# The softmax normalisation emitted two key tiles earlier, and a contiguous view for the exp, in an eight-core transformer layer

## The chip, the cores and the metric

The kernel runs on the 8 NeuronCores of one Trainium2 chip. Each core computes one sequence of 2048 tokens by 1024 features, and the cores exchange nothing. The metric is the device time in microseconds (us) of the slowest core, and the median over several executions is what counts.

## The reference

The reference adds four residual stages to x, each behind a layer norm: a holographic attention with cosines and sines (stage A), a product with the signs of a weight, a causal softmax attention with 16 heads of 64 (stage B), and the product with signs again. The change touches only stage B:

```python
Q = (x @ Wq.T + bq).reshape(b, t, H, D).transpose(0, 2, 1, 3)
K = (x @ Wk.T + bk).reshape(b, t, H, D).transpose(0, 2, 1, 3)
V = (x @ Wv.T + bv).reshape(b, t, H, D).transpose(0, 2, 1, 3)
wei = jnp.einsum('bhqd,bhkd->bhqk', Q, K) * (1.0 / math.sqrt(D))
wei = jnp.where(causal, wei, -jnp.inf)
att = jax.nn.softmax(wei, axis=-1)
out = jnp.einsum('bhqk,bhkd->bhqd', att, V)
out = out.transpose(0, 2, 1, 3).reshape(b, t, c) @ Wo.T + bo
x = x + out
```

Here t is 2048, c is 1024, H is 16 and D is 64.

## The kernel before

Everything lies transposed, with features on the 128 partitions and tokens along the free axis: XT holds x in float32, LNT the normed x in bf16, BIG the attention's output in bf16. Each stage is a function that appends instructions to a list for each engine (`Builder.op`), and the lists are emitted as they stand. There is no scheduler: the order in which the Python code calls `b.op` is the order in which each engine works, and an instruction whose semaphore has not come holds up all that stands behind it on its engine. VectorE, ScalarE and GpSimd also wait for their own instruction before.

Stage B (`emit_attnb`) takes the 16 heads as 8 pairs, p = 0 to 7, two heads one above the other on the partitions. In a pair it walks 4 query blocks of 512 queries (qs), and in a block the key tiles of 128 keys (kt): 4, 8, 12 and 16 of them, two at a time (kc). For one key tile there are:

- the scores S: two matmuls, K times Q of the two heads, into the PSUM tile PC (even kt) or PD (odd kt) (lines 890 and 895; on the diagonal also the mask, lines 902 and 904);
- the exp: one ScalarE activation of both heads, from PC or PD into one of four SBUF buffers (`do_exp`, line 934);
- the product AV: two matmuls with 64 columns of V and a column of ones, which accumulate over kt in PO0 and PO1, the two halves of the PSUM tile POB (lines 867 and 871). The column of ones makes row 64 the softmax's denominator.

AV of a pair of key tiles is issued two key tiles later than its scores. A query block ends with its last AVs. Then comes its norm (`make_norm`): for each of the two heads a Ln of the denominator (line 955) and an Exp of its negative (line 960) on ScalarE, a copy of the 64 output rows from PSUM to SBUF on VectorE (line 965), a TensorE matmul that spreads the reciprocal over 64 partitions, into the PSUM rows just copied (line 969), and the product of both into BIG (line 976). A copy of one row (line 986) closes it, and the first AV of the next block waits for that, since it writes PO0 and PO1 again. The norm is not emitted when its block ends but kept in `pending_norm` and called inside the next block's loop, in the iteration kc = 2. The norm of the very last block is called after it.

Between the scores and the AVs of each iteration one unit of the next pair's projections is issued (`make_qkv_units`), 25 in a pair: a memset of the V buffer (line 757), 4 units of Q and 4 of K (8 matmuls of 512 columns each, lines 766 and 789, evacuated by VectorE at lines 776 and 800), and 16 units of V (9 matmuls of 128 columns, lines 812 and 818, evacuated at line 827). A pair has 20 iterations. The five units left over follow its last block. Then GpSimd issues the weight loads for the pair after the next (`plan_w`, through line 214). The unit right behind the scores of kc = 0 is called U1 below, and the one of kc = 2 is U2. Where a pair changes, U1 is the memset and U2 is the first Q unit, Q0. Pair 7 has no units.

So there are 31 changes from a query block to the next: 14 in pairs 0 to 6 where U1 and U2 are Q or K units (qs 0 to 1 and 1 to 2), 7 in the same pairs where they are V units (qs 2 to 3), 6 changes of pair up to pair 6 with weights just ordered, the change from pair 6 to 7, and 3 inside pair 7.

Of the kernel before, what the change touches and what calls it, by code (L numbers as in the profile page):

```python
# [10 lines left out]
AF = mybir.ActivationFunctionType  # L11
# [64 lines left out]
def build_program(stop_after=None):  # L76
# [34 lines left out]
    with contextlib.ExitStack() as stack:  # L111
# [610 lines left out]
        def emit_attnb(ln_toks):  # L722
# [121 lines left out]
            pending_norm = [None]  # L844
            for p in range(NB):
# [5 lines left out]
                for qs in range(4):  # L851
# [5 lines left out]
                    def plan_av(kt, qs=qs, nkt=nkt, VSB=VSB,  # L857
                                av_toks=av_toks):
                        diag = kt >= 4 * qs
                        qoff = 128 * kt if diag else 512 * qs  # L860
                        N = (512 * (qs + 1) - 128 * kt) if diag else 512
                        ep = (EPA, EPB, EPC, EPD)[kt % 4]

                        def mm_av(t, kt=kt, qs=qs, ep=ep, qoff=qoff, N=N,
                                  nkt=nkt, VSB=VSB):
                            o = qoff - 512 * qs
                            t.matmul(PO0[0:65, o:o + N],  # L867
                                     VSB[:, kt * 130:kt * 130 + 65],
                                     ep[:, 0:N],
                                     start=(kt == 0), stop=(kt == nkt - 1))  # L870
                            return t.matmul(  # L871
                                PO1[0:65, o:o + N],
                                VSB[:, kt * 130 + 65:kt * 130 + 130],
                                ep[:, 512:512 + N],
                                start=(kt == 0), stop=(kt == nkt - 1))
                        wav = [exp_toks[kt]]
                        if kt == 0 and norm_done is not None:
                            wav.append(norm_done)
                        av_toks[kt] = b.op("tensor", mm_av, wait=wav,
                                           sem="T", inc=1)  # L880

                    for kc in range(0, nkt, 2):
                      for kt in (kc, kc + 1):
                        diag = kt >= 4 * qs
                        qoff = 128 * kt if diag else 512 * qs
                        N = (512 * (qs + 1) - 128 * kt) if diag else 512
                        ps = PC if kt % 2 == 0 else PD
                        def mm_s(t, ps=ps, kt=kt, qoff=qoff, N=N, diag=diag,
                                 QTp=QTp, KTp=KTp):
                            t.matmul(ps[:, 0:N],  # L890
                                     KTp[0:64, kt * 128:kt * 128 + 128],
                                     QTp[0:64, qoff:qoff + N],
                                     start=True, stop=not diag,
                                     tile_position=(0, 0))
                            ins = t.matmul(  # L895
                                ps[:, 512:512 + N],
                                KTp[64:128, kt * 128:kt * 128 + 128],
                                QTp[64:128, qoff:qoff + N],
                                start=True, stop=not diag,
                                tile_position=(64, 0))  # L900
                            if diag:
                                t.matmul(ps[:, 0:128], IDENTB[:], MASKB[:],
                                         start=False, stop=True)
                                ins = t.matmul(ps[:, 512:640], IDENTB[:],
                                               MASKB[:], start=False,
                                               stop=True)
                            return ins
                        w = list(qt_all)
                        if kt >= 2:
                            w.append(exp_toks[kt - 2])  # L910
                        elif prev_qs_exp is not None:
                            w.append(prev_qs_exp)
                        ts_ = b.op("tensor", mm_s, wait=w, sem="T", inc=1)
                        exp_toks.append([ts_, None])
                      if pending_norm[0] is not None and kc >= 2:
                          norm_done = pending_norm[0]()
                          pending_norm[0] = None
                      if pending:
                          pending.pop(0)()
                      while avq and avq[0] <= kc - 1:  # L920
                          plan_av(avq.pop(0))
                      for kt in (kc, kc + 1):
                        diag = kt >= 4 * qs
                        qoff = 128 * kt if diag else 512 * qs
                        N = (512 * (qs + 1) - 128 * kt) if diag else 512
                        ps = PC if kt % 2 == 0 else PD
                        ep = (EPA, EPB, EPC, EPD)[kt % 4]
                        wexp = [exp_toks[kt][0]]
                        if kt >= 4:
                            wexp.append(av_toks[kt - 4])  # L930
                        elif prev_qs_av is not None:
                            wexp.append(prev_qs_av)
                        def do_exp(s, ps=ps, ep=ep, N=N):
                            return s.activation(  # L934
                                ep.rearrange("p (h n) -> p h n", h=2)
                                [:, :, 0:N],
                                ps[:].rearrange("p (h n) -> p h n", h=2)
                                [:, :, 0:N], AF.Exp)
                        te = b.op("scalar", do_exp, wait=wexp, sem=None,
                                  inc=0)  # L940
                        exp_toks[kt] = te
                        avq.append(kt)
# [63 lines left out]
        for si in range(stop_idx):  # L1006
            st = STAGES[si]
            if st.startswith("ln"):
                ln_out = emit_ln(done)
                done = ln_out  # L1010
            elif st == "attna":
                done = emit_attna(ln_out)
            elif st == "ffn1" or st == "ffn2":
                done = emit_ffn(ln_out, out_dma=(st == "ffn2"))
                if st == "ffn2":
                    streamed_out[0] = True
            elif st == "attnb":
                done = emit_attnb(ln_out)
# [84 lines left out]
```

How the kernel before makes its waits and increments, by code:

```python
            def run(eng):  # L49
                hi = {}
                chain_pos = {}
                for fn, waits, sem, inc, chain in self.events[eng_name]:
                    if chain:
                        k = chain_pos.get(chain, 0)
                        if k > 0:
                            eng.wait_ge(sems[chain], k)
                        chain_pos[chain] = k + 1
                    for ws, wv in waits:
                        if wv > 0 and hi.get(ws, 0) < wv:
                            eng.wait_ge(sems[ws], wv)
                            hi[ws] = wv
                    ins = fn(eng)
                    if inc:
                        ins.then_inc(sems[sem], inc)
                    elif chain:
                        ins.then_inc(sems[chain], 1)
                return None
```

## Time and profile before

| What | us |
|---|---|
| median of 2 executions | 1731.24 (1730.67 to 1731.81) |
| the profiled execution | 1732.45 |
| its span, slowest core (core 2) | 1730.9 |
| spans of the 8 cores | 1723.2 to 1730.9 |
| stretch of stage B's attention on core 2 | some 835 to 1530 |

The span runs from the first to the last instruction of a core. The mean granted TensorE clock of the cores is 0.773 to 0.783 of full speed. PE is TensorE's matmuls, ACT is ScalarE, DVE is VectorE, POOL is GpSimd and SP is SyncE. In rows of the timeline the columns are: start in us, duration in us, engine, line, operation, output and inputs, count, and in brackets the engine's idle time before it with what ended it.

### The profile page before, as it was taken

What the parts mean: (1) busy time and instruction counts of PE and PEld (TensorE: products, weight loads), DVE (VectorE), ACT (ScalarE), POOL (GpSimd) and SP (SyncE); (2) the same over time, 40 slices, a digit from 0 to 9 for tenths busy, and PEclk for the clock granted to TensorE, in tenths of its full rate; (3) what the DMA queues carried; (4) which work ended last, traced back from release to release, by engine and by line L of the source; (5) the groups of instructions that cost most, each with busy time, mean ns of one, the idle gap of its engine ahead of it and who ended that gap; (6) DMA issues with size and microseconds to landing.
All of it is one profiled execution on the core that took longest, in us unless ns stands there. A gap on an engine that the chain in (4) does not pass through costs nothing.

```text
span 1730.9 us, 16268 instructions; the slowest of 8 cores (1723.2 to 1730.9 us)
## 1 busy us (share of the span) xinstructions
PE 1020.3 (59%) x5088; PEld 432.3 (25%) x5088; DVE 835.7 (48%) x1072; ACT 640.9 (37%) x747; POOL 56.9 (3%) x69
## 2 busy tenths in 40 slices
PE   0434343432311942961887877787878787677458
PEld 0111111110100410420433333333333333233123
DVE  1466888888898337336422223232322222125453
ACT  0535423343220051042154555554545555611400
POOL 1000000000000100001000000000000000010000
PEclk9767677675655975975988888887888887788679
DMA  9003112311000400102102020202020200022025
GB/s 244 0 1 30 23 20 37 36 12 12 0 7 6 37 1 12 37 0 26 12 1 19 1 19 1 19 1 19 1 19 1 19 1 1 1 25 25 0 64 180
DMA packets 73156, 42.03 MB, mean 24 GB/s; under 512 B 67696, under 2 KB 67696, under 8 KB 71024
## 3 DMA queue, kind: packets, MB, share of 16 engines
q0 software_dynamic: 66592, 16.78, 10.8%
q1 hardware_dynamic: 6480, 24.21, 4.5%
q8 instruction: 43, 0.70, 0.2%
q14 instruction: 41, 0.34, 0.1%
HBM read 47.28 MB, written 10.49 MB: 33 GB/s over the span
## 4 chain that ended last, share of the span: by engine, by line
PE 43%; DVE 30%; ACT 14%; issue 5%; DMA 5%; DVEq 1%; SPq 1%; POOL 1%; ACTq 0%; POOLq 0%
PE PC L624 7%; PE PC L692 5%; ACT POOLBF L934 5%; PE POB L867 4%; PE PRB L766 4%; PE POB L871 4%; PE PRB L812 3%; DVE LNT L379 3%; DVE POOLBF L374 3%; PE PRB L789 3%; ACT POOLBF L262 3%; PE PD L498 2%; DVE POOLBF L568 2%; DVE POOLBF L562 2%; DVE POOLBF L550 2%
## 5 line engine op out<-in xcount | busy, mean ns | idle before, releaser
L934 ACT ACTIVATE POOLBF<-PC 128x1024 bf16<-128x1024 f32 (+1 forms) x160 | 150.1, 938 | 308.9 <-PE PC L895 157.3
L262 ACT ACTIVATE POOLBF<-LNT 128x2048 bf16<-128x2048 bf16 x32 | 61.1, 1910 | 235.4 <-DVE LNT L256 231.3
L934 ACT ACTIVATE POOLBF<-PD 128x1024 bf16<-128x1024 f32 (+2 forms) x160 | 136.4, 853 | 24.1 <-PE PRB L818 0.4
L867 PE MATMUL POB<-POOLBF 128*65 128x512 bf16 (+1 forms) x320 | 123.8, 392 | 9.2 <-DVE PF L986 9.2
L827 DVE CAST POOLBF<-PRB 128x128 bf16<-128x128 f32 x128 | 37.7, 295 | 187.2 <-PE PRB L818 185.9
L871 PE MATMUL POB<-POOLBF 128*65 128x512 bf16 (+1 forms) x320 | 118.2, 385 | 0.0
L498 PE MATMUL PD<-LNT,WSB 128*128 128x512 bf16 x128 | 39.1, 474 | 93.5 <-ACT POOLBF L506 93.5
L283 PE MATMUL POB<-LNT,ONESB 128*1 128x512 bf16 x128 | 41.7, 485 | 86.3 <-DVE LNT L256 86.3
L624 PE MATMUL PC<-BIG,WSA 128*128 128x512 bf16 x256 | 61.4, 401 | 45.6 <-DVE BIG L580 39.9
L969 PE MATMUL POB<-PF,ONESRB 1*64 1x512 bf16 x64 | 32.5, 509 | 92.7 <-DVE PF L965 53.3
L976 DVE TENSOR_TENSOR BIG<-PF,POB 64x512 bf16<-64x512 f32 x64 | 43.5, 680 | 87.2 <-PE POB L969 87.2
L692 PE MATMUL PC<-LNT,WSA 128*128 128x512 bf16 x256 | 64.1, 413 | 22.1 <-DVE XT L702 14.0
L702 DVE TENSOR_TENSOR XT<-XT,PC 128x512 f32<-128x512 f32 x64 | 44.0, 688 | 68.3 <-PE PC L692 67.6
L498 PE MATMUL PD<-LNT,WSA 128*128 128x512 bf16 x128 | 36.1, 446 | 68.3 <-ACT POOLBF L506 68.3
L890 PE MATMUL PC<-POOLBF 64*128 64x512 bf16 (+1 forms) x160 | 61.3, 383 | 16.8 <-ACT POOLBF L934 11.6
L776 DVE TENSOR_SCALAR POOLBF<-PRB,DER 128x512 bf16<-128x512 f32 x32 | 24.0, 751 | 95.9 <-PE PRB L766 95.6
L344 PE MATMUL PRB<-PF,ONESRB 1*128 1x512 bf16 x16 | 8.5, 531 | 104.5 <-ACT PF L336 104.5
L458 PE MATMUL PC<-LNT,WSA 128*128 128x512 bf16 x128 | 41.6, 497 | 48.1 <-DMA WSA<-wv 25.8
L458 PE MATMUL PC<-LNT,WSB 128*128 128x512 bf16 x128 | 41.7, 500 | 43.6 <-DMA WSB<-wv 25.9
L890 PE MATMUL PD<-POOLBF 64*128 64x512 bf16 (+2 forms) x160 | 56.7, 355 | 16.8 <-ACT POOLBF L934 15.5
L965 DVE COPY PF<-POB 64x512 f32<-64x512 f32 x64 | 43.7, 683 | 43.7 <-PE POB L871 37.6
L895 PE MATMUL PC<-POOLBF 64*128 64x512 bf16 (+1 forms) x160 | 61.7, 385 | 0.0
(144 smaller groups left out, 2022.3 us busy)
## 6 DMA issues: line engine op xcount, KB each, us to landing
XT<-xT SPq DMA_DIRECT2D x8, 1024.0 KB, 17.5
yT<-XT SPq DMA_DIRECT2D x8, 1024.0 KB, 5.2
BIG<-wts POOLq DMA_DIRECT2D x8, 256.0 KB, 7.1
wsgn<-BIG SPq DMA_DIRECT2D x8, 256.0 KB, 2.3
WSA<-wsgn SPq DMA_DIRECT2D x8, 256.0 KB, 4.0
WSB<-wsgn SPq DMA_DIRECT2D x8, 256.0 KB, 4.4
WSA<-wk POOLq DMA_DIRECT2D x4, 256.0 KB, 5.5
WSA<-wv POOLq DMA_DIRECT2D x4, 256.0 KB, 7.3
```

Source lines behind the costliest of these rows:

```text
L262: tk = b.op("scalar", lambda s, cb=cb: s.activation(SQF[:, cb * T:(cb + 1) * T], LNT[:, cb * T:(cb + 1) * T], AF.Square), wait=[copy_toks[ ...
L374: v.tensor_tensor(SQF[:, sl], LNT[:, sl], RB[:, s4 * 512:s4 * 512 + 512], ALU.mult), wait=[e2])
L458: ins = t.matmul(PC[:, (s4 % 2) * 512:(s4 % 2) * 512 + 512], ws[:, i * 128:i * 128 + 128], LNT[:, i * T + s4 * 512: i * T + s4 * 512 + 512 ...
L498: ins = t.matmul(PD[:, (s4 % 2) * 512:(s4 % 2) * 512 + 512], ws[:, 1024 + i * 128:1024 + i * 128 + 128], LNT[:, i * T + s4 * 512:i * T + s ...
L624: ins = t.matmul(PC[:, (s4 % 2) * 512:(s4 % 2) * 512 + 512], ws[:, i * 128:i * 128 + 128], BIG[:, i * T + s4 * 512:i * T + s4 * 512 + 512] ...
L692: ins = t.matmul(PC[:, (s4 % 2) * 512:(s4 % 2) * 512 + 512], ws[:, i * 128:i * 128 + 128], LNT[:, i * T + s4 * 512:i * T + s4 * 512 + 512] ...
L766: ins = t.matmul(prr[:], ws[:, i * 128:i * 128 + 128], LNT[:, i * T + s4 * 512: i * T + s4 * 512 + 512], start=(i == 0), stop=(i == NB - 1))
L867: t.matmul(PO0[0:65, o:o + N], VSB[:, kt * 130:kt * 130 + 65], ep[:, 0:N], start=(kt == 0), stop=(kt == nkt - 1))
L871: return t.matmul(PO1[0:65, o:o + N], VSB[:, kt * 130 + 65:kt * 130 + 130], ep[:, 512:512 + N], start=(kt == 0), stop=(kt == nkt - 1))
L890: t.matmul(ps[:, 0:N], KTp[0:64, kt * 128:kt * 128 + 128], QTp[0:64, qoff:qoff + N], start=True, stop=not diag, tile_position=(0, 0))
L895: ins = t.matmul(ps[:, 512:512 + N], KTp[64:128, kt * 128:kt * 128 + 128], QTp[64:128, qoff:qoff + N], start=True, stop=not diag, tile_pos ...
L934: return s.activation(ep.rearrange("p (h n) -> p h n", h=2) [:, :, 0:N], ps[:].rearrange("p (h n) -> p h n", h=2) [:, :, 0:N], AF.Exp)
```

## The change

It has two parts. The condition `kc >= 2` goes, so that the pending norm of a block is emitted in the iteration kc = 0 of the next: behind the first two scores and ahead of U1, and on ScalarE ahead of the first two exps. And where a key tile has all 512 queries, the exp is written over `ep[:, 0:1024]` and `ps[:, 0:1024]` in place of a view with the two heads as a dimension of their own. Lines behind the second edit move by 5: in the kernel after, 934 becomes 935 or 939, 955 becomes 960, 960 becomes 965, 965 becomes 970, 969 becomes 974, 976 becomes 981 and 986 becomes 991.

```diff
-                      if pending_norm[0] is not None and kc >= 2:
+                      if pending_norm[0] is not None:
                           norm_done = pending_norm[0]()
                           pending_norm[0] = None
                       if pending:
...
-                        def do_exp(s, ps=ps, ep=ep, N=N):
-                            return s.activation(
-                                ep.rearrange("p (h n) -> p h n", h=2)
-                                [:, :, 0:N],
-                                ps[:].rearrange("p (h n) -> p h n", h=2)
-                                [:, :, 0:N], AF.Exp)
+                        if N == 512:
+                            def do_exp(s, ps=ps, ep=ep):
+                                return s.activation(
+                                    ep[:, 0:1024], ps[:, 0:1024], AF.Exp)
+                        else:
+                            def do_exp(s, ps=ps, ep=ep, N=N):
+                                return s.activation(
+                                    ep.rearrange("p (h n) -> p h n", h=2)
+                                    [:, :, 0:N],
+                                    ps[:].rearrange("p (h n) -> p h n", h=2)
+                                    [:, :, 0:N], AF.Exp)
```

**TensorE, change from qs 2 to qs 3.** Before, behind the first two scores of the new block, TensorE's row holds U1 (a V unit), the next two scores, the norm's two matmuls, U2 and the first AV:

```order
L812 MATMUL PRB<-WSB,LNT 128x128 x8
L818 MATMUL PRB<-BVR,ONESRB 128x128
L890 MATMUL PC<-POOLBF 128x512
L895 MATMUL PC<-POOLBF 128x512
L890 MATMUL PD<-POOLBF 128x512
L895 MATMUL PD<-POOLBF 128x512
L969 MATMUL POB<-PF,ONESRB 64x512 x2
L812 MATMUL PRB<-WSB,LNT 128x128 x8
L818 MATMUL PRB<-BVR,ONESRB 128x128
L867 MATMUL POB<-POOLBF 65x512
```

The same place after the change:

```order
L974 MATMUL POB<-PF,ONESRB 64x512 x2
L812 MATMUL PRB<-WSB,LNT 128x128 x8
L818 MATMUL PRB<-BVR,ONESRB 128x128
L890 MATMUL PC<-POOLBF 128x512
L895 MATMUL PC<-POOLBF 128x512
L890 MATMUL PD<-POOLBF 128x512
L895 MATMUL PD<-POOLBF 128x512
L812 MATMUL PRB<-WSB,LNT 128x128 x8
L818 MATMUL PRB<-BVR,ONESRB 128x128
L867 MATMUL POB<-POOLBF 65x512
```

The norm's two matmuls have moved ahead of U1 and of the scores of kt = 2 and 3. Nothing else moved, and nothing stands between them and U1.

**ScalarE, change from one block to the next (here into qs 2).** Before, from the last exp of the old block (a tile of 128 queries, both heads) on:

```order
L934 ACTIVATE POOLBF<-PD 128x2x128
L934 ACTIVATE POOLBF<-PC 128x1024
L934 ACTIVATE POOLBF<-PD 128x1024
L955 ACTIVATE PF<-POB 1x512
L960 ACTIVATE PF<-PF 1x512
L955 ACTIVATE PF<-POB 1x512
L960 ACTIVATE PF<-PF 1x512
L934 ACTIVATE POOLBF<-PC 128x1024
```

After:

```order
L939 ACTIVATE POOLBF<-PD 128x2x128
L960 ACTIVATE PF<-POB 1x512
L965 ACTIVATE PF<-PF 1x512
L960 ACTIVATE PF<-POB 1x512
L965 ACTIVATE PF<-PF 1x512
L935 ACTIVATE POOLBF<-PC 128x1024
L935 ACTIVATE POOLBF<-PD 128x1024
L935 ACTIVATE POOLBF<-PC 128x1024
```

The four activations of the norm have moved ahead of the new block's first two exps. The exps of full tiles stand as 128x1024 in both.

**VectorE, change of pair.** Before, from the last V casts of the old pair's iterations over the five left over to the first Q evacuations of the new one:

```order
L827 CAST POOLBF<-PRB 128x2x64 x12
L757 MEMSET POOLBF 128x2080
L965 COPY PF<-POB 64x512
L976 TENSOR_TENSOR BIG<-PF,POB 64x512
L965 COPY PF<-POB 64x512
L976 TENSOR_TENSOR BIG<-PF,POB 64x512
L986 COPY PF<-PF 1x512
L776 TENSOR_SCALAR POOLBF<-PRB,DER 128x512 x2
```

After:

```order
L827 CAST POOLBF<-PRB 128x2x64 x13
L970 COPY PF<-POB 64x512
L981 TENSOR_TENSOR BIG<-PF,POB 64x512
L970 COPY PF<-POB 64x512
L981 TENSOR_TENSOR BIG<-PF,POB 64x512
L991 COPY PF<-PF 1x512
L757 MEMSET POOLBF 128x2080
L776 TENSOR_SCALAR POOLBF<-PRB,DER 128x512
```

The memset has moved behind the norm's five operations; the thirteenth cast is that of qs 3's first iteration, which used to stand ahead of the norm before it.

## Rows read from the trace of the kernel before

**Rows 1.** The page: span, and granted TensorE clock in 40 slices.
```profile
span 1730.9 us, 16268 instructions; the slowest of 8 cores (1723.2 to 1730.9 us)
...
PEclk9767677675655975975988888887888887788679
```
**Rows 2.** Busy time by windows, attention of stage B (window: us, busy by engine, PEclk).
```profile
835.00:1530.00 695.00, 540.31 (x3224) 243.47 (x3221) 195.91 (x355) 364.39 (x448) 17.55 (x20) 0.83 0.08 8
```
**Rows 3.** Waits in 850 to 1525 (who, for whom: us, times, longest).
```profile
PE POB L969 <- DVE PF L965: 51.6, 30, 1.7
PE POB L969 <- ACT PF L960: 37.4, 32, 1.7
```
**Rows 4.** Timeline, pair 1, change from qs 2 to qs 3.
```profile
989.91 0.22 PE L871 MATMUL POB<-POOLBF 128*65 128x128 bf16 x1
...
990.55 1.02 ACT L934 ACTIVATE POOLBF<-PC 128x1024 bf16<-128x1024 f32 x1 [1.39 <-PE PC L895]
...
992.83 0.59 ACT L955 ACTIVATE PF<-POB 1x512 f32<-1x512 f32 x1
...
992.89 0.37 PE L890 MATMUL PD<-POOLBF 64*128 64x512 bf16 x1 [0.78 <-ACT POOLBF L934]
...
994.45 0.37 PE L969 MATMUL POB<-PF,ONESRB 1*64 1x512 bf16 x1 [1.17 <-ACT PF L960]
...
996.55 0.60 PE L969 MATMUL POB<-PF,ONESRB 1*64 1x512 bf16 x1 [1.72 <-DVE PF L965]
...
997.08 1.03 PE L812 MATMUL PRB<-WSA,LNT 128*128 128x128 bf16 x8
...
998.74 0.61 PE L867 MATMUL POB<-POOLBF 128*65 128x512 bf16 x1 [0.41 <-DVE PF L986]
```
**Rows 5.** Timeline, the norm behind the very last block.
```profile
1521.46 0.22 PE L871 MATMUL POB<-POOLBF 128*65 128x128 bf16 x1
...
1523.39 0.37 PE L969 MATMUL POB<-PF,ONESRB 1*64 1x512 bf16 x1 [1.71 <-ACT PF L960]
...
1525.48 0.60 PE L969 MATMUL POB<-PF,ONESRB 1*64 1x512 bf16 x1 [1.72 <-DVE PF L965]
```
**Rows 6.** Timeline, pair 1, change from qs 1 to qs 2.
```profile
967.84 0.22 PE L871 MATMUL POB<-POOLBF 128*65 128x128 bf16 x1
...
968.53 1.90 PE L789 MATMUL PRB<-LNT,WSA 128*128 128x512 bf16 x8
...
975.29 3.21 PE L789 MATMUL PRB<-LNT,WSA 128*128 128x512 bf16 x8
...
978.34 0.38 PE L867 MATMUL POB<-POOLBF 128*65 128x512 bf16 x1
```
**Rows 7.** Busy time by windows, the same place (PEclk is the third number from the end).
```profile
968.00:974.00 6.00, 3.51 (x19) 1.12 (x17) 2.18 (x4) 4.48 (x6) 0.00 (x0) 1.00 0.01 3
974.00:978.00 4.00, 3.24 (x8) 1.16 (x9) 1.71 (x3) 2.05 (x2) 0.00 (x0) 0.57 0.02 4
```
**Rows 8.** Timeline, change from pair 1 to pair 2.
```profile
1020.27 1.79 DVE L757 MEMSET POOLBF<- 128x2080 bf16 x1 [0.57 <-DVE POOLBF L827]
...
1020.83 0.22 PE L904 MATMUL PD<-MASKB,IDENTB 128*128 128x128 bf16 x1
...
1021.57 0.90 POOL L214 DMA_DIRECT2D WSB<-wvbT  x1
...
1026.66 0.60 PE L969 MATMUL POB<-PF,ONESRB 1*64 1x512 bf16 x1 [1.72 <-DVE PF L965]
...
1029.70 3.30 PE L766 MATMUL PRB<-LNT,WSB 128*128 128x512 bf16 x8 [2.44 <-DMA WSB<-wvbT]
```
**Rows 9.** Timeline, pair 7, change from qs 2 to qs 3.
```profile
1496.79 0.22 PE L871 MATMUL POB<-POOLBF 128*65 128x128 bf16 x1
...
1505.84 0.61 PE L867 MATMUL POB<-POOLBF 128*65 128x512 bf16 x1 [1.59 <-DVE PF L986]
```
**Rows 10.** Groups of ACT by line and shape.
```profile
L934 ACT ACTIVATE POOLBF<-PC 128x1024 bf16<-128x1024 f32 x128 | 131.0, 1023 | 287.8 <-PE PC L895 157.3 <-PE PC L904 124.9
```

## The prediction, written before the changed kernel ran

> **What bounds the kernel now.** I read the page first, then the busy time by windows of stage B's attention, its waits, and last the timeline around single changes of query block. The page gives a span of 1730.9 us and shows TensorE's granted clock at 0.8 or 0.9 in most slices of the stage [rows 1]. The stage takes 695 us: TensorE is busy 540 us of it, ScalarE 364 us, and the mean clock is 0.83 [rows 2]. Since the clock has two levels, 1.2 and 2.4 GHz, 0.83 means that the lower one holds for about a third of the stage. So TensorE is the bound, and it loses time by idling and by the low clock that follows. Where does it idle? The waits name the norm's matmul: 51.6 us for VectorE's copy and 37.4 us for ScalarE's Exp, 89 us together in 62 waits [rows 3]. That is the largest idle time of TensorE in the stage, and the change moves just this piece.
>
> The timeline shows why one norm costs so much. Take the change of pair 1 from qs 2 to qs 3 [rows 4]. The last AV starts at 989.91 and ends its columns at 990.13, which I call +0. ScalarE then starts two exps (the first at +0.4), and the Ln of the norm stands behind them and starts only at +2.7, though the sums that it reads were there at +0. The norm's first matmul starts at +4.3, the second at +6.4, and the next AV at +8.6. The two matmuls are 2.1 us apart because VectorE copies the second head only after it has multiplied the first, and the AV is 2.2 us behind the second matmul because it waits for the closing copy (line 986), not for data. On this core 6 of the 7 changes with V units take 8.6 us from AV to AV, one 8.5; the 14 with Q or K units take 10.0 to 10.7, as the one at 968.06 does (978.34 less 968.06 is 10.3) [rows 6].
>
> **The exp's view.** The order of instructions shows the full tiles as 128x1024 before and after, so the old view was already folded into one row of 1024 elements. It takes 1023 ns before [rows 10]. I cost this edit at 0. As bounds I take 20 ns either way on each of the 224 full tiles, 4.5 us if all of them lay on the path; they do not, as ScalarE has 330 us of slack in the stage [rows 2].
>
> **The norm moved.** What does it take without the two exps ahead of it? The trace has that case: behind the very last block the norm is called at once. AV ends at 1521.68 (start 1521.46 and 0.22), and the matmuls start at 1523.39 and 1525.48, so at +1.7 and +3.8 in place of +4.3 and +6.4 [rows 5]. The norm is 2.6 us earlier. But U1 and the scores of kt = 2 and 3, which used to fill TensorE while the exps and the Ln ran, now stand behind it. What counts is TensorE's idle time between the last AV and the next, kind by kind. I count it from where a matmul has taken in its columns (0.22 us for 512 of them at 2.4 GHz, the distance of two AVs), not from the end that the row shows (0.37), since the next can start there.
>
> *14 changes with Q or K units.* Before, TensorE works to about +3.0 (two scores 0.45, U1 1.8, two scores), with 0.24 idle between the last two scores. It idles 1.3 to the first matmul at +4.3 and 1.9 to the second, 3.45 in all. After, it works to +0.5, idles 1.2 to +1.7 and 1.9 to +3.8, 3.1 in all, and then U1, scores and U2 follow without a gap: the exps of kt = 0 and 1, now behind the norm on ScalarE, end by +5.2 (four activations to +3.0, two exps of 1.1), while U1 ends at +6 or later. The gain is 0.33 us each, 4.6 us. Bounds: with both units at 2.4 GHz AV would start at 3.8 + 0.2 + 1.75 + 0.45 + 1.75 = +7.95, a gain of 2.3; with both at 1.2 GHz at 3.8 + 0.4 + 3.4 + 0.85 + 3.4 = +11.9, a loss of 1.6. One of two units is slow now (1.90 against 3.21 us [rows 6]), so I stay near the idle account.
>
> *7 changes with V units.* V units are short, so the exps lie open today. TensorE idles 0.4 and 1.0 ahead of the scores of kt = 2 and 3, which wait for an exp each (0.78 for the second by the row's own count), 1.3 and 1.9 ahead of the norm's matmuls, and 0.4 ahead of AV: 5.1 in all [rows 4]. After, idle is again 3.1. The gain is about 1.95 us each. Worked by AV's start, the V unit takes 1.2 us slow (997.08 to 998.3, line 812 and the bias behind it) and 0.7 fast: 3.8 + 0.4 + 1.2 + 0.85 + 1.2 = +7.5 slow. Fast it would be +5.9, and there the closing copy decides at 3.8 + 2.2 = +6.0. Against +8.6 this is 1.1 to 2.6 us [rows 4]. I take 1.9, 13.3 us.
>
> *3 changes in pair 7.* There are no units, so AV follows the closing copy: +6.0 for a change whose AV now starts at 1505.84 less 1497.01 = +8.8 [rows 9]. 2.7 us each, 8.1 us; half of it if the exps take it back.
>
> *The change from pair 6 to 7.* Like pair 1 to 2, but without a load to wait for. Ln and Exp are done while the five left-over V units run. The first scores end at 1021.05 and the first matmul follows, the second 2.1 us later at 1023.2 in place of 1026.66 [rows 8]. That is 3.5 us once; the two scores that follow take about 1 us and fit in the 2.2 us of the closing copy.
>
> *6 changes of pair.* There Q0 waits for its weights: the load is issued at 1021.57, behind the last left-over unit, and lands for 1029.70, with TensorE idle 2.44 us [rows 8]. The norm gets 3.5 us earlier and TensorE waits that much longer for the same load. Nothing is gained; what hides the edit is the transfer. GpSimd's row is not moved past anything.
>
> The wait that the change adds is that of the norm's matmuls ahead of U1. Behind them stand U1, two scores and U2; VectorE's evacuation of U1 waits with them, but the next unit writes the other half of PRB, so it holds nobody.
>
> **Sum.** 4.6 + 13.3 + 8.1 + 3.5 + 0 = 29.5 us. The profiled execution took 1732.45 us, 1.55 more than its span and 1.2 more than the median. 1732.45 less 29.5 is 1703; less 1.2, so that it compares with the median of 1731.24, 1702.
>
> **The clock.** It is full to about 974.5 and at its lower level until about 978 (0.57 as a mean over 974 to 978) [rows 7]: after the two idle times of the norm TensorE runs a few us of its work at 1.2 GHz. The idle pattern after the change is the same as in the Q and K cases, and more compact in the V cases and in pair 7. So I value the clock at 0, but it is the main unknown: a slow stretch that is longer or shorter by 3.4 us of busy time (the 974.5 to 978 piece) is worth 1.7 us at each of 24 changes. The Trainium skill's page "TensorE: Matmul & The Clock Gate", section "HAM oscillation — how this bites in real kernels", says that idle gaps throttle the array and that the work behind them then starts cold, again and again. The trace agrees, with 3.21 us for a unit behind the gap and 1.90 ahead of it. By that rule alone U1 and both scores, now behind the gap, would be slow as well, which is the third case below.
>
> **The rivals.**
>
> - *The clock gains too.* The idle pieces of V changes and of pair 7 come closer together and the slow stretch gets shorter by 3.4 us in half of the 24 changes and a bit more: 14 times 1.7 is 24 more, 1678. For it: the V changes idle 5.1 us now and 3.1 after. Against it: the Q and K changes have hardly less idle time.
> - *The clock takes it back.* U1, the scores and U2 all run at 1.2 GHz in the 14 Q and K changes, 1.7 us each: 29.5 less 24 leaves 6, 1726. For it: there is now more work right behind the gap. Against it: what ran slow behind U2 before is fast instead.
> - *The exps bind.* ScalarE's order between AVs is full with 4 activations and 4 exps, and the V blocks and pair 7 are near its rate of one exp in 1.1 to 1.2 us. Half of 13.3 and 8.1 is lost: 1713.
> - *Slower than before.* In all 24 changes the slow stretch grows by one piece of 3.4 us of busy time: 24 times 1.7 is 41, less 29.5 is 11 more, 1743. It decides once 17 or more of them grow so. It would take two such pieces each to pass 2%.
> - *The loads land earlier.* At a change of pair the memset (1020.27 to 1022.06) now lies beside GpSimd's issues and after the change behind the norm [rows 8]. If it had held the issues up, six loads would come up to 1.8 us earlier: 11 more, 1691. The Trainium skill's page "SBUF — State Buffer", section "SBUF: two separate sides", says that a VectorE operation in a two-port mode keeps GpSimd from writing descriptors. The trace does not show it: the issue beside the memset takes 0.90 us like the others.
>
> **How the numbers follow.** Forecast 0.47, clock gains 0.22, clock takes back 0.13, exps bind 0.10, slower 0.05, loads earlier 0.03. About 2% is what a measurement of this kernel can tell from no change; that is 34.6 us, so "faster" starts below 1696.6. The forecast's own spread is some 10 us, and a quarter of it (0.11) lies there; with the 0.22 and most of the 0.03 it makes 0.35. Slower by over 2% is the tail of one case, 0.02, which leaves 0.63 for within 2%. The range goes from 1684, between the forecast and the clock's gain, to 1724, near the case in which the clock takes it back.
>
> **What would show it.** Right: the norm's matmuls at +1.7 and +3.8 behind the last AV, AV to AV at about 10.0 (Q, K), 7 (V) and 6.0 (pair 7), Q0 waiting for its weights 4 to 6 us in place of 2.4, a mean clock still near 0.83 over the stage, exps at 1023 ns. Wrong: matmuls later than that (another wait has taken over), a clock away from 0.83 by more than 0.02, changes of pair that get shorter, or a gap ahead of the scores of kt = 2 and 3 that waits for an exp.

## The result and the profile after

The kernel after takes 1709.2 us (median of 7, 1705.9 to 1713.0) against 1731.6 us (median of 6, 1729.6 to 1732.8) for the kernel before on the same chip. The ratio is 0.9872 with a 95% interval of 0.9857 to 0.9886: 22 us or 1.3% faster. The forecast was 1702, range 1684 to 1724. In some executions of these programs the cores of one die run at a lower clock and take some per cent longer; they count in the medians given here and not in the ratios.

The head of the page and the granted clock in 40 slices, of the kernel after; they answer to [rows 1]:

```profile
span 1710.7 us, 16270 instructions; the slowest of 8 cores (1683.3 to 1710.7 us)
...
PEclk9867677675655985975897888887878788788679
```

The clock looks as before. What is new is in the first line: the cores lie 27 us apart, where it was 8 us before. The list of the cores' spans of the same execution (core: span, mean clock):

```profile
core 0: 1710.6 us, clock 0.776
core 1: 1710.7 us, clock 0.773
core 2: 1683.3 us, clock 0.784
core 3: 1692.3 us, clock 0.779
...
core 6: 1710.7 us, clock 0.780
```

Over the 8 executions of the kernel after with spans for each core, the mean of all cores is 1697.5 us, and the slowest and the fastest core of an execution are 21.7 us apart on average. Over 30 executions of the kernel before, on the three chips of the later runs, they are 1725.5 and 8.7 us. So a core gains 28 us on average, and the slowest of eight, which is the metric, gains 22. Which cores are slow changes from one execution to the next.

The timeline of the change from qs 2 to qs 3 in pair 2 on core 6, which has the longest span; it answers to [rows 4]. The last AV of the old block ends at 1068.95:

```profile
1068.88 0.39 PE L890 MATMUL PC<-POOLBF 64*128 64x512 bf16 x1
...
1069.05 0.59 ACT L960 ACTIVATE PF<-POB 1x512 f32<-1x512 f32 x1 [1.06 <-PE POB L871]
...
1070.67 0.37 PE L974 MATMUL POB<-PF,ONESRB 1*64 1x512 bf16 x1 [1.18 <-ACT PF L965]
...
1072.76 0.60 PE L974 MATMUL POB<-PF,ONESRB 1*64 1x512 bf16 x1 [1.72 <-DVE PF L970]
...
1073.29 1.03 PE L812 MATMUL PRB<-WSB,LNT 128*128 128x128 bf16 x8
...
1074.47 0.60 PE L890 MATMUL PC<-POOLBF 64*128 64x512 bf16 x1
...
1075.44 1.04 PE L812 MATMUL PRB<-WSB,LNT 128*128 128x128 bf16 x8
...
1076.62 0.64 PE L867 MATMUL POB<-POOLBF 128*65 128x512 bf16 x1
```

The Ln starts 0.1 us behind the last AV and the norm's matmuls at +1.7 and +3.8, as forecast from [rows 5]. Nothing in this change waits for an exp. But all that follows runs at 1.2 GHz: the V units take 1.03 and 1.04 us for their 8 matmuls (0.62 at full clock), the scores 0.60 (0.39), and the next AV starts at +7.7. The busy time by windows shows the clock of this piece (the third number from the end, 0.50 of full speed):

```profile
1073.00:1077.00 4.00, 4.00 (x24) 2.06 (x24) 1.59 (x4) 2.74 (x4) 0.00 (x0) 0.50 0.00 0
```

In the kernel before, only the second V unit stood behind the norm. The first, in the change of [rows 4], stood ahead of it and ran at full clock:

```profile
990.60 0.62 PE L812 MATMUL PRB<-WSA,LNT 128*128 128x128 bf16 x8
```

The 7 changes of this kind on core 6 average 7.67 us against 8.59 before.

A change with Q units, from qs 0 to qs 1 in pair 2, same core. The last AV starts at 1027.81 and ends at +0 = 1028.03; it answers to [rows 6]:

```profile
1027.81 0.22 PE L871 MATMUL POB<-POOLBF 128*65 128x128 bf16 x1
...
1031.83 0.60 PE L974 MATMUL POB<-PF,ONESRB 1*64 1x512 bf16 x1 [1.72 <-DVE PF L970]
...
1032.36 3.59 PE L766 MATMUL PRB<-LNT,WSB 128*128 128x512 bf16 x8
...
1036.86 2.31 PE L766 MATMUL PRB<-LNT,WSB 128*128 128x512 bf16 x8
1039.01 0.38 PE L867 MATMUL POB<-POOLBF 128*65 128x512 bf16 x1
```

U1 is slow from end to end (3.59 us against 1.90), U2 in part, and AV starts at +11.0, later than before. It is fast then (0.38 us), while before the AVs behind such a change ran slow. The same change in the kernel before, whose second Q unit and first AV were:

```profile
1041.04 3.59 PE L766 MATMUL PRB<-LNT,WSB 128*128 128x512 bf16 x8
1044.42 0.63 PE L867 MATMUL POB<-POOLBF 128*65 128x512 bf16 x1
```

So the slow stretch has moved forward, from U2 and the AVs to U1, the scores and a part of U2.

The change from pair 1 to pair 2, same core, with the memset, the issue of the last weight load and Q0; it answers to [rows 8]:

```profile
1014.00 0.90 POOL L214 DMA_DIRECT2D WSB<-wvbT  x1
...
1015.53 0.37 PE L974 MATMUL POB<-PF,ONESRB 1*64 1x512 bf16 x1 [1.72 <-DVE PF L970]
...
1017.91 1.79 DVE L757 MEMSET POOLBF<- 128x2080 bf16 x1 [0.57 <-DVE PF L991]
1023.09 3.19 PE L766 MATMUL PRB<-LNT,WSB 128*128 128x512 bf16 x7 [6.38 <-DMA WSB<-wvbT]
```

The norm is done before the load is; TensorE then idles 6.38 us without a break, and Q0 comes 9.1 us behind the issue. In 850 to 1500 the waits of TensorE (who, for whom: us, times, longest) are these; they answer to [rows 3]:

```profile
PE POB L974 <- DVE PF L970: 53.3, 31, 1.7
...
PE POB L974 <- ACT PF L965: 28.1, 24, 1.5
...
PE PRB L766 <- DMA WSB<-wvbT: 17.3, 3, 6.4
PE PRB L766 <- DMA WSA<-wvbT: 16.5, 3, 6.0
```

The wait for weights has grown to 33.8 us over six changes; in the kernel before the same two rows say 7.3 and 7.5 us, 14.8 in all. The norm's own wait fell only from 89 to 81 us, and 1.7 us of that is a wait of the very last norm, which lies in the window of before and not in this one. It is hardly shorter, it stands elsewhere.

### The profile page after: what moved, and what is told of

The parts are those of the page before. It is cut to its first block, busy times and chain, and to the rows that moved or that the text cites. A ratio compares the mean times of both kernels' runs of the same rounds, so it can differ in the third digit from the quotient of the medians.

```text
span 1710.7 us, 16270 instructions; the slowest of 8 cores (1683.3 to 1710.7 us)
## 1 busy us (share of the span) xinstructions
PE 1007.3 (59%) x5031; PEld 429.0 (25%) x5088; DVE 835.5 (49%) x1072; ACT 640.9 (37%) x747; POOL 56.9 (3%) x69
## 3 DMA queue, kind: packets, MB, share of 16 engines
q0 software_dynamic: 66592, 16.78, 11.2%
## 4 chain that ended last, share of the span: by engine, by line
PE 46%; DVE 29%; ACT 11%; issue 5%; DMA 5%; DVEq 1%; SPq 1%; POOL 1%; ACTq 0%; POOLq 0%
PE PC L624 7%; PE PC L692 6%; PE PRB L766 5%; PE POB L867 4%; PE PRB L812 4%; PE PRB L789 4%; PE POB L871 4%; DVE LNT L379 3%; DVE POOLBF L374 3%; ACT POOLBF L262 3%; PE PD L498 2%; PE PC L890 2%; DVE POOLBF L550 2%; DVE POOLBF L568 2%; DVE POOLBF L543 2%
## 5 line engine op out<-in xcount | busy, mean ns | idle before, releaser
L935 ACT ACTIVATE POOLBF<-PC 128x1024 bf16<-128x1024 f32 x128 | 131.0, 1023 | 162.7 <-PE PC L895 80.1
L935 ACT ACTIVATE POOLBF<-PD 128x1024 bf16<-128x1024 f32 x96 | 98.2, 1023 | 14.4 <-PE PRB L818 0.4
L974 PE MATMUL POB<-PF,ONESRB 1*64 1x512 bf16 x64 | 28.2, 440 | 84.8 <-DVE PF L970 55.0
L960 ACT ACTIVATE PF<-POB 1x512 f32<-1x512 f32 x64 | 37.7, 589 | 101.0 <-PE POB L871 98.0
L890 PE MATMUL PC<-POOLBF 64*128 64x512 bf16 (+1 forms) x160 | 64.6, 404 | 6.2 <-DVE POOLBF L827 5.2
L895 PE MATMUL PC<-POOLBF 64*128 64x512 bf16 (+1 forms) x160 | 64.8, 405 | 0.0
```

Of the source, the lines that this page charges most:

```text
L890: t.matmul(ps[:, 0:N], KTp[0:64, kt * 128:kt * 128 + 128], QTp[0:64, qoff:qoff + N], start=True, stop=not diag, tile_position=(0, 0))
L935: return s.activation(ep[:, 0:1024], ps[:, 0:1024], AF.Exp)
```

## The experiments

**The view of the exp alone.** The second edit as in the diff of the change, with the condition as before:

```diff
+                        if N == 512:
+                            def do_exp(s, ps=ps, ep=ep):
+                                return s.activation(
+                                    ep[:, 0:1024], ps[:, 0:1024], AF.Exp)
...
```

> Only the second edit: the exp over a contiguous view, the norm where it was. Both theories (the gain is all from the norm's place; the view helps too) differ here: by the first the ratio to the kernel before is 1.000 within 0.001 and the 1024-element exps stay at 1023 ns; by the second a part of the 22 us shows here, at least 3 us, with a shorter exp.

Measured: 1731.7 us, ratio 0.9992 (0.9960 to 1.0024), and the exps at 1024 ns. The first theory holds: the view is worth nothing that this run can tell, and the exp is as long as before.

**The norm early in pair 7 alone.**

```diff
-                      if pending_norm[0] is not None and kc >= 2:
+                      if pending_norm[0] is not None and (kc >= 2
+                                                          or p == NB - 1):
```

> The kernel before with the norm at kc = 0 in pair 7 alone, so in 4 of the 31 changes of block: into pair 7 and 3 inside it. Theory (places add up, and these four, with neither units nor a load behind them, give their full idle time back): 3.8 for the change into pair 7 (13.0 to 9.2) and 3 times 2.9 (8.8 to 5.9), 12 to 13 us, ratio about 0.993. Rival (the exps take part of it back, as ScalarE is nearly full in pair 7): 6 us or less.

Measured: 1721.1 us, ratio 0.9930 (0.9899 to 0.9960), so 12 us. The change into pair 7 takes 9.4 us and the three inside 6.1 on average. The exps take nothing back.

**The norm early in pairs 0 to 6 alone.**

```diff
-                      if pending_norm[0] is not None and kc >= 2:
+                      if pending_norm[0] is not None and (kc >= 2
+                                                          or p < NB - 1):
```

> The kernel before with the norm at kc = 0 in pairs 0 to 6 alone, 27 of the 31 changes. Idle account of the prediction: 4.6 + 13.3 = 18 us less, ratio 0.990. Theory now (on the cores that come last, the low clock and the wait for the weights take back what the shorter idle times give, so a pair lasts 85.3 us as before): 8 to 10 us less, ratio 0.994 to 0.995, with the cores spread over more than 15 us and the last of them at 85.3 us per pair.

Measured: 1724.5 us against 1733.1, ratio 0.9929 (0.9887 to 0.9971), so 9 us by the medians, 12 by the ratio, and 5 to 20 by its interval. The interval is wide, since the cores spread; in the profiled execution:

```profile
core 1: 1702.4 us, clock 0.787
core 2: 1700.5 us, clock 0.787
...
core 4: 1722.9 us, clock 0.775
core 5: 1723.0 us, clock 0.774
```

The mean core is at 1705.7 us over 4 executions, 20 below the 1725.5 of before; the slowest core is at 1718.8, 11 below its 1730.1. So the prediction's sum of idle times, the idle account (18), is near the mean core's gain, and the theory of the take-back fits the slowest. On core 4 the Q changes take 10.85 us and V changes 7.67; on core 2 10.0 and 7.66. The two kernels with half the change each come to 0.9930 times 0.9929 = 0.986, the whole change to 0.987: the parts add up within their intervals. The spread comes with pairs 0 to 6: slowest and fastest core are 20.9 us apart on average here and 10.2 with pair 7 alone, where the kernel before has 11.2 on the same chip.

**Fillers: TensorE kept busy in the norm's gaps.** The kernel after, with matmuls whose results are never read, so this kernel does more than the reference asks:

```diff
+            def plan_fill(n):
+                half = (24 - len(pending)) % 2 if pending else 0
+                prr = PR if half == 0 else PR2
+                def mm_fill(t):
+                    for _ in range(n):
+                        ins = t.matmul(prr[:], LNT[:, 0:128], LNT[:, 0:512],
+                                       start=True, stop=True)
+                    return ins
+                b.op("tensor", mm_fill, wait=[pr_free[half]], sem="T", inc=1)
...
+                                if pending or p == NB - 1:
+                                    plan_fill(5 if hh == 0 else 8)
                                 tr1 = b.op("tensor", lambda t, po=po,
```

> The kernel after, with matmuls added whose results nobody reads (512 columns each, into the half of PRB that is free): 5 ahead of the norm's first matmul and 8 ahead of its second, at every change of block. They fill 1.1 and 1.7 us of TensorE's idle 1.2 and 1.9. Theory (the low clock behind the norm is what takes the gain back): U1, the scores and U2 run at 2.4 GHz, AV to AV falls from 9.9 to 11 to about 8.0 in the Q and K changes and from 7.7 to 6.0 to 6.3 in the V changes, mean clock of the stage up from 0.83 to 0.88 or more, 1665 to 1685 us. Rival (the exps or the closing copy bind there anyway): within 6 us of the kernel after. Slower than the kernel after, 1715 or more, if fillers run at the low clock and push the norm's matmuls back.

Measured: 1661.3 us, ratio 0.9595 (0.9576 to 0.9614), 4 us below the theory's range. The timeline of the first Q change of pair 1 on core 0; L851 are the fillers, L986 the norm's matmuls, L877 is AV, and the last AV before ended at 938.36:

```profile
940.08 0.37 PE L986 MATMUL POB<-PF,ONESRB 1*64 1x512 bf16 x1
940.39 1.90 PE L851 MATMUL PRB<-LNT 128*128 128x512 bf16 x8
...
942.22 0.40 PE L986 MATMUL POB<-PF,ONESRB 1*64 1x512 bf16 x1
942.55 1.90 PE L766 MATMUL PRB<-LNT,WSA 128*128 128x512 bf16 x8
...
944.92 1.90 PE L766 MATMUL PRB<-LNT,WSA 128*128 128x512 bf16 x8
...
946.65 0.38 PE L877 MATMUL POB<-POOLBF 128*65 128x512 bf16 x1
```

The norm stands where it stood, at +1.7 and +3.9; both units take 1.90 us, and AV starts at +8.3. On this core Q and K changes average 8.3, V changes 6.48 us. The busy time by windows of core 0 (the third number from the end is the clock):

```profile
860.00:1390.00 530.00, 499.82 (x3172) 230.10 (x3171) 169.22 (x306) 316.00 (x388) 15.78 (x18) 0.96 0.10 10
```

The clock is 0.96 in place of the 0.83 that the kernel after has there. The fillers compute nothing and the norm's matmuls start no earlier, so the 48 us (44 on the mean core) are the price of the low clock. The wait for the norm itself, 81 us in the kernel after, is still the larger one.

**The same fillers on the kernel before.** The same two pieces of code, with the norm at kc = 2.

> The kernel before (norm at kc = 2) with the same added matmuls as in the run with fillers on the kernel after: 5 and 8 of them ahead of the norm's two. With the clock held up on both sides the two runs differ by the norm's place alone. Idle account of the prediction: 0.33 times 14, 1.9 times 7, 2.7 times 3 and 3.5, so 29.5 us between them, this one at 1687 to 1693 us. Rival (with the clock up the place of the norm is worth little, and the measured 22 us were mostly a matter of the clock): within 12 us of the 1661 of that run.

Measured: 1676.1 us, ratio 0.9690 (0.9675 to 0.9705). The two differ by 15 us (16 by the ratios), half of the idle account, and yet each kind of change but one comes out as it says, on the slowest core of each (core 4 here and core 0 there), in us:

| Change | norm at kc = 2 | norm at kc = 0 | saved | idle account |
|---|---|---|---|---|
| Q | 8.53 | 8.29 | 0.24 | 0.33 |
| K | 8.65 | 8.34 | 0.31 | 0.33 |
| V | 8.45 | 6.48 | 1.97 | 1.9 |
| into pair 7 | 13.0 | 9.2 | 3.8 | 3.5 |
| in pair 7 | 9.04 | 6.41 | 2.6 | 2.7 |
| change of pair | 15.45 | 16.78 | -1.3 | 0 |

The last row is the exception: with the norm late, its matmuls and fillers end just ahead of Q0; with it early TensorE idles through the rest of the load. Neither theory as I had put it is right: the place of the norm is worth what the account says where TensorE is kept going, and costs 1.3 us where it is not, 8 us over six. The rows sum to 29.4 less 8. Another 5 us are lost between the changes, and the traces show where: 4.2 in the first block of a pair, right behind the change of pair. Its eight AVs take 1.03 us with the norm late, in all six pairs, and up to 2.03 with it early, since they still run at the low clock there. The first AV behind Q0 in pair 2, with the norm late (the first line, core 4) and early (the second, core 0):

```profile
1016.29 0.38 PE L877 MATMUL POB<-POOLBF 128*65 128x512 bf16 x1
...
1014.51 0.63 PE L877 MATMUL POB<-POOLBF 128*65 128x512 bf16 x1
```

So the unbroken wait for the load costs twice, 8 us in its length and 4 in what runs slow behind it. With both, and a last 0.6 us in pair 7, the stretches of the two cores differ by 16 us.

**Early loads on the kernel before.** The weight buffer of a pair is read out before the pair starts, so its next load can be issued then:

```diff
                 QTp, KTp, VSB = QT2[pi], KT2[pi], VSB2[pi]
+                free_ws[pi] = b.tok("T")
+                plan_w(p + 2)
...
                 pair_end_T[pi] = b.tok("T")
-                free_ws[pi] = b.tok("T")
-                plan_w(p + 2)
```

> The kernel before, with the weight loads for the pair after the next issued at the start of a pair (its weight buffer is already read by then) and not at its end. Q0 then waits for no load. Theory: the norm's second matmul becomes the last thing ahead of Q0, at about 11 us behind the last AV in place of 13.5 to 14.2, so 2.4 to 3 us at each of 6 changes of pair, 15 to 18 us, ratio 0.990. If the low clock takes that back as well, 0.995 or more.

Measured: 1718.8 us, ratio 0.9939 (0.9923 to 0.9955), 11 us, less than expected. A change of pair takes 14.55 us in place of 15.8 to 17.2, so 1.2 to 2.6 us less (means of one core each) and not 2.4 to 3: the norm at kc = 2 takes the load's place, and the Q unit behind it is still slow.

**Early loads on the kernel after.** The same edit.

> The kernel after with the same early loads. The prediction said that at the 6 changes of pair the load hides 3.5 us of earlier norm. Theory: Q0 starts at 9 us behind the last AV in place of 13.8, 4.5 to 5 us each, 27 to 30 us less than the kernel after and ratio 0.970 to 0.972 to before; against the run with early loads on the kernel before, the norm's move is now worth 30 us or more in place of 22. Rival (the change of pair is held by something else, or the clock takes it back): less than 15 us below the kernel after.

Measured: 1666.7 us, ratio 0.9635 (0.9619 to 0.9650), 42 us below the kernel after, where 27 to 30 were expected, and 52 below the early loads on the kernel before. The norm's move is worth more than twice as much once no load stands behind it. The change from pair 1 to 2 on core 1; the last AV ended at 1002.4, L976 is the norm's second matmul and L869 AV:

```profile
1009.66 0.60 PE L976 MATMUL POB<-PF,ONESRB 1*64 1x512 bf16 x1 [1.72 <-DVE PF L972]
...
1011.26 3.62 PE L766 MATMUL PRB<-LNT,WSB 128*128 128x512 bf16 x8
...
1014.67 0.63 PE L869 MATMUL POB<-POOLBF 128*65 128x512 bf16 x1
```

A change of pair takes 11.9 us, 5.5 less than on core 6 of the kernel after: 33 us over six. What goes beyond the expectation is clock: the Q changes average 9.4 us in place of 10.9 (10 us over seven), of which the K changes take 3 back, and the eight AVs behind a change of pair take 1.3 us in place of 1.9. And the spread is gone:

```profile
core 1: 1663.5 us, clock 0.788
core 2: 1657.8 us, clock 0.785
```

These are the slowest and the fastest of the eight, 5.7 us apart. So the cores drift apart only where they wait for the loads.

**The norm split around U1.** Ln, Exp and both copies first, then U1, then matmuls and products:

```diff
-                          norm_done = pending_norm[0]()
+                          norm_done = pending_norm[0](
+                              pending.pop(0) if pending else None)
                           pending_norm[0] = None
-                      if pending:
+                      elif pending:
                           pending.pop(0)()
...
+                                parts.append((hh, po, RECB, OSCR, r1, c1))
+                            if unit is not None:
+                                unit()
+                            for hh, po, RECB, OSCR, r1, c1 in parts:
                                 tr1 = b.op("tensor", lambda t, po=po,
```

> The kernel after with the norm split on TensorE and VectorE: Ln, Exp and both copies of the norm are emitted first, then U1, and then the two matmuls and products. U1 fills TensorE's first idle time, and the second copy no longer waits for the first product. Theory (TensorE's idle time and the clock that it brings down are the whole price): the second matmul at 3.1 us behind the last AV in place of 3.8, idle time in a Q or K change 0.8 us in place of 3.1, the clock stays up in most, AV to AV 8 to 8.5 and 6.5 in V changes: 1665 to 1680 us. Rival (idle time counts, but the clock falls all the same): 14 times 2.3 and 7 times 1.2, but slow, 1685 to 1695.

Measured: 1683.9 us, ratio 0.9739 (0.9721 to 0.9756), 25 us below the kernel after, at the edge between both. The norm's second matmul comes at +3.2. AV comes at 8.5 to 9.1 in the Q and K changes and at 7.1 in the V changes (averages of each core). The mean clock of the cores is 0.786 to 0.791 against 0.773 to 0.787: a smaller gap saves its own length, but the clock still falls in many of them.

**The norm early only at the six changes of pair with a load.**

```diff
-                      if pending_norm[0] is not None and kc >= 2:
+                      if pending_norm[0] is not None and (kc >= 2
+                              or (qs == 0 and 1 <= p < NB - 1)):
```

> The kernel before with the norm at kc = 0 only at the 6 changes of pair with a load. The prediction valued these at 0, since the load hides the norm. Theory now: 0 to 3 us slower, ratio 1.000 to 1.002, since the norm no longer breaks TensorE's wait for the load, and Q0 follows a longer unbroken idle time. Rival (the memset beside the loads' issue held them up, and its new place brings the loads earlier): 6 us or more faster, with Q0 starting at least 1 us sooner behind the issue of the load.

Measured: 1731.9 us against 1729.9, ratio 1.0022 (0.9993 to 1.0051). The interval holds 1, so that it costs anything is not shown; that it gains nothing is. Q0 starts 6.9 to 7.5 us behind the issue on the eight cores here (mean 7.2) and 6.6 to 8.3 in the kernel before (mean 7.7): half a microsecond less where the rival wanted at least 1, and no time gained. The run shows one thing more. TensorE's waits for the six loads are 22 to 26 us here against 6 to 16 before (22 to 34 in the kernel after), and yet the cores lie no further apart (3.8 to 7.8 us in eight of the nine executions that count, 26.6 in the other): the longer wait alone does not drive the cores apart.

**Fillers and early loads together, on the kernel after.**

> The kernel after with both the added matmuls and the early loads. Theory (two separate prices: the low clock, and the wait for the weights in which the norm's gain is lost): with the load gone the 6 changes of pair fall from 15 to 17 us to about 11, so 25 to 33 us below the 1661 of the fillers alone, 1628 to 1636. Rival (they are one price, and the fillers have already taken it): 1650 or more.

Measured: 1620.9 us, ratio 0.9374 (0.9357 to 0.9391), 40 us below the fillers alone and beyond what I expected. The eight cores lie between 1616.4 and 1618.5 us. A change of pair takes 11.1 us in place of 15.0 to 17.2, and the eight AVs behind it 1.03 us on every core. Low clock and load are two prices.

**The split norm with early loads and fewer fillers.**

> The run before this one, with the norm split as well (U1 between the norm's first and second half; fewer added matmuls, 0 and 2 in Q and K changes, 3 and 5 in V changes, 5 and 5 in pair 7). The second exp behind the norm ends at 5.3 us and then bounds the scores: AV at 5.3 + 0.2 + 1.75 = 7.3 in Q and K changes in place of 8.3, little in V changes. About 15 us less: 1612 to 1620. If the clock falls while TensorE waits for the exps, 1630 or more.

Measured: 1621.0 us in the middle one of the three executions that count in the ratio, against the same runs of the kernel before, ratio 0.9376 (0.9359 to 0.9392), the same as without the split. The expected 15 us did not come. Its cores' mean clock is 0.811 to 0.818 against 0.828 to 0.835; the changes of pair fall from 11.1 to 10.3 us, the K changes rise from 8.3 to 8.6 and more. Since the split and the fewer fillers came in one run, their shares are not told apart.

**The split norm with early loads and no fillers.**

> The split norm with early loads and no added matmuls, which leaves nothing in that does no work. By the split alone (1684) less 30 to 35 us for 6 changes of pair without a load to wait for: 1649 to 1655, cores within 8 us of each other. If the spread of the cores stays over 15 us, it does not come from the loads.

Measured: 1647.2 us, ratio 0.9523 (0.9506 to 0.9540), and the cores within 6 us. This is the best version without idle matmuls: 83 us below the kernel before on the same chip and 62 below the kernel after. With fillers it is the run with 1620.9 us, 6.3% below before.

## Why the prediction was right, and where it was not

The mechanism was the forecast's: the norm's matmuls at +1.7 and +3.8, the exps behind them without effect on TensorE, the view worth nothing, Q0 waiting the longer for its load. The time is inside the range, and the gain is 22 us for 29.5. The 7 us between them are no noise: two terms of the sum are too high, those of the V changes and of the changes of pair.

Term by term, from the timelines of the slowest profiled core each (core 2 before, core 6 after), where the stretch from the first to the last norm of stage B went from 661.7 to 640.8 us:

- *Pair 7*: 8.1 forecast, 3 times 2.8 = 8.4 measured. *Into pair 7*: 3.5 and 3.8. The run with these four alone gave 12 us for 11.6.
- *Q and K changes*: 4.6 forecast. AV to AV went from 10.30 to 10.91 in the Q changes and from 10.26 to 9.91 in the K changes, 1.8 us lost over 14. But the blocks behind them got shorter, by 5.9 us over the seven Q changes and 2.1 over the K changes; 0.85 us a time is what four AVs at full clock in place of the lower one come to. Together 6 us won: somewhat more than said, and not in the place where it was said to show (AV at 10.0 in both).
- *V changes*: 13.3 forecast, 6.4 measured (7 times 0.92), and 2.4 more in the blocks behind them. This term was mis-sized. The prediction worked out 7.5 for a slow change and 6.0 for a fast one and took a value between, since the idle account said so. Each one is slow: 7.67 on core 6, averages of 7.59 to 7.67 on all eight. The idle account assumes that the clock does what it did. But before, only the second V unit stood behind the gap (0.62 and 1.03 us), and here the first unit, the scores and the second unit all run at 1.2 GHz. With the clock held up by fillers the same step measures 1.97 us.
- *Changes of pair*: 0 forecast, 6 us lost: 6 times 0.3 in the changes themselves and 4 us behind them, where the eight AVs of the first block take 1.93 us in place of 1.26 on average. The transfer hid the norm, as said. What was left out is that the norm had broken TensorE's wait, and that more of what follows would then run slow. This is the second term that was mis-sized.

These terms, less 0.6 us lost between the changes of pair 7, come to the 20.9 us by which the stretch got shorter. In the rivals one sum is slightly off: 29.5 us of loss at 1.7 us each take 18 changes and not 17.

What the prediction had not in it at all is the spread. It worked on one core and took the slowest to be like the others, as in the kernel before, where they lie 9 us apart on average. After the change the mean core gains 28 us, near the sum of 29.5, and the slowest of eight 22. In the profiled execution cores 0, 1, 6 and 7 wait 8.2 to 8.7 us from issue to Q0 and cores 2 to 5 6.7 to 7.05; the first have 85.3 to 85.4 us from pair to pair (means of pairs 1 to 6) and Q changes of 10.9 to 11.0, the others 81.4 to 83.1 and 9.3 to 10.4. That a load lands later explains only a part: between core 6 and core 2 the six changes of pair make 10 us of the 24 by which their stretches differ. The Q changes make 11, of which the K changes give 3 back, and the AVs behind the changes of pair 5; all of these are the clock. Nor is the difference between the loads new: in the kernel before they reach their reader in 6.6 to 8.3 us, and all eight cores have 85.4 to 86.1 us from pair to pair. That the wait for the loads is needed for the spread is shown by the runs with early loads (5.7 us of spread, and 2 us with fillers), and that the longer wait is not enough by the run with the early norm at the changes of pair alone. Why a load lands later on one core than on another, why it does so for a whole execution, and why so many cores come to 85.3 us a pair, stays open; no run looked at it.

Of the rivals, "the clock takes it back" holds for the Q changes of the slow cores, where U1 takes 3.59 us, and in the V changes, which the prediction had not counted there. "The clock gains too" holds for some changes of cores 2 to 5: on core 2 three of seven Q changes take 8.2 us, with both units at 1.90, though the K change behind such a one takes 10.9 to 11.1 in place of 9.9. The Trainium skill ("TensorE: Matmul & The Clock Gate", section "HAM oscillation — how this bites in real kernels") says that work behind a wait starts cold, every time. The traces agree for the V changes, where all seven run slow behind the gap, and not for the Q changes, where three of seven on core 2 do not; the fillers put the price at 48 us of the kernel after. The exps do not bind in the kernel after: TensorE's scores wait 8 us for them in all, 27 before. The memset beside the issues costs nothing that can be measured.

## What to carry to other kernels

Where short idle times bring the clock down, count for each the work that runs slow behind it, and not its own length alone: here a sum of idle times was right where the clock was held up and no load stood behind, and half of it was left at the V changes, where the move put more work behind the gap. A step that is moved out of the cover of a transfer gains nothing until the transfer itself goes, so look first whether its issue waits for something that it need not. And where the metric is the slowest of several cores, read the cores' spread before and after: a change can drive them apart and give the mean core more than the metric.

## What the runs showed of the hardware that I had not expected

- 13 matmuls of 512 columns that nobody reads, 2.8 us of work in gaps of 1.2 and 1.9 us, raise the clock of stage B from 0.83 to 0.96 and take 48 us off; the same on the kernel before takes 53 us off.
- The same program on eight cores with equal work gives spans from 1683 to 1711 us in one execution, and the order of the cores is another in the next. The same load, issued within some 3 us on all cores (at 928 to 931), reaches its reader in 6.8 to 7.4 us on four cores and in 8.2 to 9.1 on the other four.
- A wait of 2.44 us for a load, when nothing breaks it any more, is a wait of 6.38: six such waits went from 14.8 to 33.8 us in all while the time fell. The eight AVs behind the load run slow for longer as well, 1.93 us on average for 1.26.
